# A graph network kernel: how far the scatters of edge counts stand behind the gathers of the edge loop

## The reference

```
x_i = ssp(ssp(x) @ W_i.T + b_i);   x_j = ssp(ssp(x) @ W_j.T + b_j)
msg = x_j[dst] * (edge_attr @ W_att.T)
m   = x_i + segment_sum(msg, src)
...                                  # three residual layers, a gate
x   = layernorm(x + that)
alpha = <q[dst], k[src]> / 8;  a = softmax of alpha over the edges of one dst
out = segment_sum(a * v[src], dst), mean of the heads, + x @ ws + bs     (twice)
x   = layernorm(x + that)
```

## Time and profile before

| | |
|---|---|
| median of three runs | 3566.74 us |
| the profiled execution | 3568.79 us |
| its span in the profile | 3567.0 us |
| PE busy | 3189.7 us, 89% |
| DVE busy | 2898.0 us, 81% |
| POOL busy | 2667.4 us, 75% |
| POOL's indirect DMAs: scatters L476, gathers L467 | 752 (in the loop) and 588, 1613 and 991 ns each |
| edge loop on PE: sums, L1295 | 11760 matrix products, 1707.5 us |

### The profile page before, as it was taken

The page is one execution under the profiler, slowest core; times in us unless marked ns, Lnnn a source line. Parts: engine busy times, 40 slices in busy tenths (PEclk is TensorE's granted clock), DMA queues, the critical chain, the costliest instruction groups (busy, mean ns, idle before and its releaser), DMA issues.

```text
span 3567.0 us, 64347 instructions
## 1 busy us (share of the span) xinstructions
PE 3189.7 (89%) x20040; PEld 1823.8 (51%) x20040; DVE 2898.0 (81%) x8886; ACT 999.1 (28%) x1689; POOL 2667.4 (75%) x1764
## 2 busy tenths in 40 slices
PE   4989999999999999999999999976788888899996
PEld 2666666666666666666666666642222222322222
DVE  5788888888888888888888888868677775877886
ACT  3111111111111111111111111133455554233433
POOL 2288888888888888888888888861787888476874
PEclk6999999999999999999999999987899999999998
DMA  8733333333333333333333333315544452332320
GB/s 277 280 50 48 44 47 49 50 49 49 50 46 43 49 50 50 49 50 46 43 49 50 49 49 49 39 2 148 150 132 146 132 151 72 80 89 76 89 64 9
DMA packets 265753, 271.38 MB, mean 76 GB/s; under 512 B 145252, under 2 KB 224717, under 8 KB 265673
## 3 DMA queue, kind: packets, MB, share of 16 engines
q1 hardware_dynamic: 87751, 162.29, 15.3%
q0 software_dynamic: 131712, 19.76, 13.0%
q10 hardware_dynamic: 46210, 88.29, 8.2%
HBM read 189.11 MB, written 81.07 MB: 76 GB/s over the span
## 4 chain that ended last, share of the span: by engine, by line
POOL 47%; PE 19%; issue 16%; DMA 6%; DVE 6%; ACT 3%; SPq 2%; POOLq 1%; DVEq 0%; ACTq 0%
POOL edge_counts L476 27%; POOL nodes_and_gaps L467 14%; PE PS L1396 6%; PE PS L1419 6%; DMA edge_counts<-small 4%; POOL scores L531 4%; PE PS L1428 3%; SPq L395 2%; POOL counts_and_logs L514 1%; DVE scores L1134 1%; DVE PS L1145 1%; DVE counts_and_logs L1120 1%; PE PS L1408 1%; DMA edge_counts<-counts_and_logs 1%; ACT scores L721 1%
## 5 line engine op out<-in xcount | busy, mean ns | idle before, releaser
L1295 PE MATMUL PS<-scores 128*128 128x320 bf16 x11760 | 1707.5, 303 | 127.0 <-DVE scores L966 70.5
L1295 PEld LDWEIGHTS PS<-scores 128*128 128x128 bf16 x11760 | 1156.1, 99 | 660.1 <-DVE scores L966 153.0
L476 POOL DMA_INDIRECT edge_counts<-small x752 | 1213.1, 1613 | 275.4 <-issue 275.4
L531 POOL TENSOR_TENSOR scores<-scores,max_of_targets 125x896 f32<-125x896 f32 x335 | 701.8, 2143 | 191.2 <-ACT max_of_targets L716 141.8
L467 POOL DMA_INDIRECT nodes_and_gaps<-xj_rows,small x588 | 582.5, 991 | 248.6 <-issue 161.3
L966 DVE TENSOR_SCALAR scores<-scores,small 128x192 bf16<-128x192 bf16 x3136 | 748.1, 304 | 3.4
L881 DVE SCALAR_TENSOR_TENSOR scores<-scores,small,PS 128x512 bf16<-128x512 f32 x784 | 573.0, 731 | 0.0
L1134 DVE TENSOR_TENSOR scores<-PS,counts_and_logs 125x896 f32<-125x896 f32 x350 | 377.8, 1082 | 203.9 <-PE PS L1396 76.6
L616 ACT ACTIVATE scores<-nodes_and_gaps 128x512 bf16<-128x512 f32 x98 | 61.7, 630 | 1392.4 <-DVE nodes_and_gaps L944 848.0
L721 ACT ACTIVATE scores<-scores 125x896 f32<-125x896 f32 x350 | 329.8, 948 | 372.9 <-POOL scores L531 366.0
L1396 PE MATMUL PS<-q_features,k_features 64*125 64x448 f32 x1400 | 371.1, 612 | 67.9 <-DVE scores L1134 65.0
(11 more groups left out here) (192 smaller groups left out, 2125.0 us busy)
## 6 DMA issues: line engine op xcount, KB each, us to landing
counts_and_logs<-edge_counts SPq DMA_DIRECT2D x70, 980.0 KB
scores<-tile_keys ACTq DMA_DIRECT2D x96, 512.0 KB
edge_counts<-counts_and_logs SPq DMA_DIRECT2D x50, 766.0 KB
edge_counts<-counts_and_logs SPq DMA_DIRECT2D x35, 980.0 KB
running_max<-fetch_targets ACTq DMA_DIRECT2D x48, 312.5 KB
max_of_targets<-fetch_targets ACTq DMA_DIRECT2D x48, 312.5 KB
edge_counts<-small POOLq DMA_INDIRECT x752
nodes_and_gaps<-xj_rows,small POOLq DMA_INDIRECT x588
```

The lines of the kernel that those rows point to most:

```text
L476: pool.indirect_dma_start(cnt_dram, bass.IndirectOffsetOnAxis(ap=index[:, s:s + 1], axis=0), value[:, s:s + 1], None, compute_op=ALU.add). ...
L531: nc.gpsimd.tensor_tensor(t, t, MB, ALU.subtract).then_inc(sem("shifted"), 1)
L1295: ins = nc.tensor.matmul(PS[:, b, 0:HI * F], onehot[:, s, b * P:b * P + 128], spread[:, s, i].rearrange("p h f -> p (h f)"), start=first a ...
```

## The change

The loop is cut in four segments at the group pairs 13, 25 and 37, thus at groups 26, 50 and 74. In the segments the scatters stand 4, 5, 6 and 7 groups behind the gathers. The step from one distance to the next is made by the first group of a segment, which issues its six gathers and no scatter. What is not scattered in the loop is left for the tail: seven groups there, 56 scatters, in place of four and 32. On POOL and DVE each segment is two unrolled groups (where the distance changes) and a hardware loop over the rest. DVE copies the counts for the new distance, and into the buffer that goes with it. PE, ACT and SP have the same instructions as before.

```diff
 BEHIND = 4
+STEPS = (13, 25, 37)
+STARTS = (BEHIND // 2,) + STEPS
+ENDS = STEPS + (NG // 2,)
+LATEST = BEHIND + len(STEPS)
...
-            def group(g, u, scatters):
+            def group(g, u, behind):
                 pool.wait_ge(sem("targets_staged"), g + 1)
-                if scatters:
-                    pool.wait_ge(sem("counts_staged"), 2 * (g - BEHIND) + 2)
+                if behind is not None:
+                    pool.wait_ge(sem("counts_staged"), 2 * (g - behind) + 2)
                 settled()
                 for s in range(0, G, ROUND):
-                    if scatters:
+                    if behind is not None:
                         for e in range(ROUND):
-                            scatter(g - BEHIND, s + e, cidx[u], cnt[u])
+                            scatter(g - behind, s + e, cidx[(u + behind) % 2], cnt[(u + behind) % 2])
...
             for g in range(BEHIND):
-                group(g, g % 2, False)
+                group(g, g % 2, None)
             pool.wait_ge(sem("counts_cleared"), 16 * FILLS)
-            with pool.Fori(BEHIND // 2, NG // 2) as k:
-                for u in range(2):
-                    group(2 * k + u, u, True)
+            for j, (first, end) in enumerate(zip(STARTS, ENDS)):
+                group(2 * first, 0, None if j else BEHIND)
+                group(2 * first + 1, 1, BEHIND + j)
+                with pool.Fori(first + 1, end) as k:
+                    for u in range(2):
+                        group(2 * k + u, u, BEHIND + j)
             pool.wait_ge(sem("indexed"), 2 * NG)
-            for h in range(NG - BEHIND, NG):
+            for h in range(NG - LATEST, NG):
...
-                if counts is not None:
-                    stage_counts(g + 2 - BEHIND, u, counts)
+                if behind is not None:
+                    stage_counts(g + 2 - behind, (u + behind) % 2)
...
-            with dve.Fori(BEHIND // 2, NG // 2 - 1) as k:
-                for u in range(2):
-                    edge_group(2 * k + u, u, k, counts=False)
+            for j, (first, end) in enumerate(zip(STARTS, ENDS)):
+                edge_group(2 * first - 2, 0, first - 1, None if j else BEHIND)
+                edge_group(2 * first - 1, 1, first - 1, BEHIND + j)
+                with dve.Fori(first, end - 1) as k:
+                    for u in range(2):
+                        edge_group(2 * k + u, u, k, BEHIND + j)
```

More of the change, by code:

```diff
@@ L863, in stage_targets, with stage_counts @@
                 nc.vector.tensor_copy(dcur[u], dst_i[:, bass.ds(g * G, G)]).then_inc(sem("targets_staged"), 1)
-            def stage_counts(h, u, first):
-                if not first:
+            def stage_counts(h, u):
+                if not isinstance(h, int) or h > 1:
                     dve.wait_ge(sem("count_added"), 16 * G * (h - 1))
@@ L932, in match_low, with compute @@
                 nc.vector.tensor_scalar(onehot[:, s, :], iota_h, los[:, s:s + 1], None, ALU.is_equal).then_inc(sem("low_matched"), 1)
-            def compute(g, u, k, first, counts, last, end):
+            def compute(g, u, k, first, behind, last, end):
                 sl = bass.ds(g * G, G)
@@ L1017, in _, with edge_group @@
                     take_fifth(0, f, h, 0)
-            def edge_group(g, u, k, first=False, counts=None, last=False, end=False):
+            def edge_group(g, u, k, behind, last=False, end=False):
                 if not end:
                     stage_keys(g + 1)
-                compute(g, u, k, first, counts, last, end)
-            for g in range(BEHIND):
-                edge_group(g, g % 2, g // 2, g == 0, None if g < BEHIND - 2 else g == BEHIND - 2)
-            with dve.Fori(BEHIND // 2, NG // 2 - 1) as k:
-                for u in range(2):
-                    edge_group(2 * k + u, u, k, counts=False)
+                compute(g, u, k, isinstance(g, int) and g == 0, behind, last, end)
+            for g in range(BEHIND - 2):
+                edge_group(g, g % 2, g // 2, None)
+            for j, (first, end) in enumerate(zip(STARTS, ENDS)):
[4 more added lines that the diff above has]
+                        edge_group(2 * k + u, u, k, BEHIND + j)
             for u in range(2):
-                edge_group(NG - 2 + u, u, NG // 2 - 1, last=True, end=u == 1)
+                edge_group(NG - 2 + u, u, NG // 2 - 1, None, last=True, end=u == 1)
             dve.wait_ge(sem("tile_summed"), G * NG)
```

## The result

The changed kernel takes 3608.68 us (3605.51 to 3623.21, four runs) beside 3567.3 us of the kernel before: 1.0121 times as long, 95% interval 1.0104 to 1.0139. It is slower, as forecast, but by 41 us in place of 27. The profiled execution took 3607.94 us, 39.15 more than that of before, with a span of 3606.1.

What follows compares the result with a forecast made beforehand. The edge loop was taken to go at POOL's pace, with DVE caught by late PE reports. Profiled 3568.79 us plus 37.0 for the tail minus 10 gained gave 3595.8, or 3594 after 2.05 off to the median; range 3557 to 3607.

Steps and rivals of the forecast that it cites:

- Scatters out of the loop: POOL in the loop: a group of six gathers takes 7.74 us instead of 23.07, saving 45.9 us over three groups.
- the hold: Loop: PE's reports near POOL's switch from gathers to scatters reach DVE only 3.6 us behind it; inferred.
- What DVE makes of it, G: Loop time DVE gains from POOL's saving: 3.8 us per skip, 11.4 in all, taken as 10; bounds -3 to 45.9.
- the end of its lead: Loop: POOL's lead over DVE can grow by only 19 us, making the third skip nearly worthless.
- The tail: Behind the loop: 24 more scatters make six rounds of 9.43 us, 56.6 us more.
- Its tie to DVE's last group: Tail start: the first scatter is freed by DVE's last group, whatever lead POOL has.
- The slack: Beside the tail, before attention: 19.6 us of other work covers later counts, leaving 37.0 us lost, bounds 35 to 39.
- The forecast's further 3 us: Attention behind the tail: up to 3 us more if PE's clock has dropped in a longer pause.
- Nothing else: Longer loop code entered four times, and DVE's count copies: taken as 0 us, bounds 0 to 4.
- B (full catch-up): Loop: DVE is bound by gathers' arrival and follows POOL fully, G 45.9 us, 3557.8 us total; chance 0.19.

Runs made afterwards that it cites:

- e15: Kernel before with the scatters of groups 0 to 93 left out, six gathers in a row, on chip 7 with late reports, single run: 3475.2 us.
- e13: The whole changed kernel, unaltered, against the kernel before on chip 7 with late reports: 3613.0 beside 3569.2 us, ratio 1.0118.
- e14: Changed kernel with each of three steps spread over two groups, at most three gathers in a row, against before on chip 7: 3593.6 us, 1.0067.
- e11: Changed kernel with only the step at pair 13, against before on chip 9 with late reports: 3570.9 us, ratio 1.0009.
- e12: One step only, spread over groups 26 and 27, at most three gathers in a row, against before on chip 9: 3565.4 us, 0.9994.
- e1: Loop of the kernel before plus 24 more tail scatters, against before on chip 4: 3600.1 us, 1.0114.
- e3: Changed kernel's four segments, all at distance 4, no group without scatters, against before on chip 4: 3564.6 us, 1.0011.
- e6: Kernel before, unchanged, run again on chip 5 without late reports: 3563.2 us.
- first comparison: Changed kernel against the kernel before, chip not known, late reports in both traces: 3608.7 beside 3567.3 us, ratio 1.0121.
- e5: Changed kernel, unaltered, run again against before on chip 5 without late reports: 3562.7 beside 3563.2 us, 0.9995.
- e17: Kernel before with each round reordered to two scatters, a gather, two scatters, two gathers, against before on chip 8: 3577.8 us, 1.0032.
- e9: Kernel before with gathers left out from group 4 on, scatters kept, on chip 14 without late reports, single run: 3413.4 us.
- e10: Kernel before with scatters of groups 0 to 93 left out, gathers kept, on chip 14 without late reports, single run: 3397.3 us.

## Why the prediction was wrong

The sign was right, and so was the way to it: a loop that doesn't follow POOL, and a longer tail behind it. It was luck, too, that the comparison ran in the regime of the trace that the forecast read: on chips 5 and 14 the same kernel follows POOL. The time was outside the range by 1.7 us, and the forecast was of 27 us more where 41 were measured. By its own steps:

1. *Scatters out of the loop.* Right. POOL's group of six gathers lasts 7.5 us where the forecast had 7.74, and on a chip without the hold POOL's saving arrives at DVE nearly whole (40.8 of 45.9 us).
2. *What DVE makes of it, G: the step that failed.* Forecast 10 us, measured 2.8. The forecast took the hold for something that stands at POOL's going over from gathers to scatters, and so counted a group without scatters as one with fewer holds. e15 shows late reports with gathers alone. A step as the change makes it puts three and six gathers in a row, and DVE idles 7.8 to 8.8 us beside them, PE breaks up and its clock falls. That costs 4.5 to 7.5 us at each step (the trace) and 19.4 us for three (e13 against e14); for one, e11 against e12, 7.3 us at the step and 2.4 at the loop's end. How the length of a hold follows from the row is not settled, as e15's six cost less each time than nine. The other half of the argument held: DVE lags behind POOL afterwards, POOL reaches the end of its lead (37.1 us of waiting, 4.5 of them behind the first step already), and without the long rows a step gives about 5 us.
3. *The tail.* Six rounds more at 9.43 us were forecast, 56.6; measured 59.1. Of the 2.5 us 1.4 are longer rounds, 9.59 us, and the rest is that the first scatter starts 0.74 us behind the last message, where it had started 0.43 before it. Its tie to DVE's last group was right.
4. *The slack.* 19.6 us forecast, 19.5 measured. Behind it the attention took 2.3 us more. ACT waits for its second and third block too, 2.87 and 1.79 us in the rows above, where before they lay ready. That this is the cause isn't shown, and e1 speaks against it: with the same tail, on chip 4, its attention takes 1124.4 us, less than before's 1126.6. Over all traces the stretch lies between 1124.4 and 1133.7 us, so 2.3 is within what it varies by. The forecast's further 3 us, for a clock that drops in the longer pause, no run shows: over the attention's first 200 us the granted clock is 0.85 before and 0.89 after.
5. *Nothing else.* Right within what e3 can tell, 0 to 8 us.

Sum of the misses: 7.2 + 2.5 + 2.3 = 12.0, of 39.1 - 27. The medians lie 2.3 us further apart than the profiled executions, 41.4.

The range failed by other terms than the forecast's time did. G was given -3 to 20, and 2.8 lies inside; with it and 37.0 for the tail the time would be 3600.9, inside too. But the slow end, 3607, took the tail at 37.0 without the bounds that steps 4 and 5 had given it (35 to 39, up to 3 more, 0 to 4), and tail, slack and attention together measured 59.1 - 19.5 + 2.3 = 41.9.

A part of the price of a row of gathers was there to be read. At the start POOL issues six at once for groups 2 and 3, and the messages beside them, at 77.87, 100.44 and 122.91 us of that trace, are 22.57 and 22.47 us apart, where 21.41 follow without a gather. The first of the two is no sign of the hold, as e6 has 22.31 there on a chip without it. The second is one, about 1 us: e6 has 21.42. e11, on a chip with the hold, has 21.42 as well, so the sign doesn't always show.

Of the rivals, B (full catch-up) was wrong for the first comparison. On chips 5 and 14 its mechanism holds: the changed kernel follows the gathers, with 40.8 of the 45.9 us (e5). Its time, 3557.8, is near the 3562.7 and 3558.5 us there only because the kernel before is faster too: against that B had said 8.9 us less, and 0.5 and 2.5 less were measured, level with before. The time of a gather on such a chip is 2.3 us and more, 2.5 in the middle, from its start to its landing (e6), and L944 waits for the gathers in every group there. The rule of the Trainium skill that spoke for B ("DMA: Bandwidth & Descriptors", "Anatomy of one DMA — SWDGE (gpsimd) path") has about 2.0 us for a GpSimd DMA; e6 is near it, and where they differ the measured 2.5 decides. What no one could read from one chip's trace is that the two regimes exist. Why chips 7, 8 and 9 have the hold and 4, 5 and 14 don't stays open. The runs without it all stand between the first comparison and those of chips 9, 7 and 8, and each chip was used at one time only, so no run tells a property of the chip from one of the time.

## What to carry to other kernels

Work taken from the engine that sets the pace is a gain only if the next one can follow: look for where its wait ends, and whether that is the work that you took away or something that stands beside it. What moves out of a loop loses the cover that it had there; price it at the other end before counting the gain (15.3 us saved and 18.9 paid, of which a slack of 19.6 pays once). And a result near 1% on one chip can be another on the next: run before and after on more than one before explaining it.

## What the runs showed of the hardware

- In some runs PE's semaphores come late while POOL issues indirect gathers and shortly behind them: ended at 1209.93, acted on at 1217.66, in a row of nine. In the kernel before, with rows of three, the largest lateness of a report with its own rise is 4.1 us, in e15 with rows of six 3.1 us, in e17 with rows of one and two 1.0 us. Chips 7, 8 and 9 and the first comparison show it, in 10 to 42% of PE's reports; three other chips show none. DVE idled up to 9.6 us for it in one piece (e11).
- Where PE breaks up into single products beside a row of nine gathers, its granted clock falls to the lower level for 6.8 to 10.2 us. In the loop (to 2250 us) the clock is 1.00 in e5 and e6, 0.98 in both traces of the first comparison.
- Without gathers the two kinds of chip run this loop alike within 0.7 us in 3413, one run each. The kernel before is 3560.0, 3561.1 and 3563.2 us on the chips without the hold and 3566.4, 3566.5 and 3569.2 on those with it, 0.2% apart; the changed kernel against it 1.0118 and 1.0121 with the hold, 0.9991 and 0.9995 without.
- PE's floor of a group of edges is 21.4 us against POOL's 23.0: some 150 us over the loop for whoever takes work from POOL without paying for it in the tail (e9 is 148 us faster than before, e10 164, with work left out).
